# Stacking the query and key operands of an attention stage through scratch memory instead of through on-chip copies

## The chip, the cores and the metric

The kernel runs on one core of one Trainium2 chip. The metric is the device time in microseconds (us). Before the change it is 1969.96 us, the median of three runs (1965.92 to 1970.75). Since there is one core, its span and its clock are the whole picture.

## What is computed

The reference is one gated cross-attention block. Cut to what matters here:

```
x = x + tanh(g_xattn) * attention(layernorm(x), ctx, ctx, heads=16)
x = x + tanh(g_ffn)   * ffn(layernorm(x), w_gate, w_up, w_down)

attention: q, k get rotary position factors;
           scores = q k^T / sqrt(32) + slope[h] * (column - row)
           softmax over columns, times v
ffn:       weights quantized to 4 bits in blocks of 32, activations to 16 bits
```

x and ctx are 4 x 1024 x 512 in float32, with 16 heads of 32 columns each.

## The kernel before

The program is written out engine by engine, with semaphores between them. It has an attention stage (to about 1040 us) and then the feed-forward stages.

Attention works on 16 groups (`p`), each with four heads of one batch element, in the code's words a group's `K` and `Q` parts (`w` = 1 and 0). A group has two halves of 512 query rows, and each half has 8 steps of 128 keys, so a group takes 16 steps (numbered w = 0 to 15 below) and the stage 256. The softmax needs each row's maximum before it starts. So beside the scores of step g (`score`, line 852) TensorE already computes the products for the row maxima of a later half (`row_max`, line 839), 11 steps ahead; VectorE reduces them (line 1205). The maxima of the next group begin at step 5 of this one.

A score is wanted in nearly float32 accuracy, while TensorE gets float16 operands. So q and k are split in a high and a low float16 part (`hi`, `lo`), and the matmul's 101 rows are a stack: rows 0 to 31, 32 to 63 and 64 to 95 hold hi/hi, hi/lo and lo/hi of q and k, rows 96 to 99 the position bias, row 100 the negated maxima. `QA` and `KA` are these stacks.

How a stack comes about: TensorE transposes four heads at once (`turn`, line 826; K of the next group at step 0, Q of the group after the next at step 8). The result has the four heads below each other on 128 partitions. ScalarE writes `hi` (line 1011), VectorE `lo` (line 1220). Then the transfer queue of SyncE moves each head's 32 partitions to the three places in its stack (`stack`, lines 583, 584 and 588): seven transfers a head, at steps 1, 2, 3 and 4 of the group before. `write_rows` (line 595) writes the maxima's row at steps 4 and 12, and they are needed from steps 8 and 0 on. SyncE works strictly in program order, so each of its waits holds back all transfers written behind it.

In `QA` and `KA` there are two sets of buffers, and a set has two tensors with two heads each. A semaphore of a head (`d_st`) tells TensorE that its seven transfers are there.

Of the kernel before, what the change touches and what calls it, by code (L numbers as in the profile page):

```python
# [104 lines left out]
class Step:  # L105


    def __init__(self, g):
        self.g = g
        self.hf, self.s = hf, s = g // 8, g % 8  # L110
        self.p, self.qc = p, qc = hf // 2, hf % 2
        w = 8 * qc + s
        self.inside = 0 <= hf < NHALF
        m = g + 8 + LEAD
        self.hm, self.im = m // 8, m % 8
        self.maxima = 0 <= self.hm < NHALF
# [12 lines left out]
        if 0 <= p and p + 2 < NQ and w in (0, 2, 6, 8, 10, 14):
            k = (0, 2, 6, 8, 10, 14).index(w)  # L130
            self.rope = (p + 2, k // 3, k % 3)
        elif -10 <= g <= -5:
            self.rope = (1, (g + 10) // 3, (g + 10) % 3)
        self.add = hf - 1 if s == 4 and 1 <= hf < NHALF else None
        self.norm = []
        if 2 <= p + 3 < NQ:
            self.norm += [(p + 3, i) for i in NORM_TILES.get(w, ())]
        if g < -7:
            self.norm += [(1, 2 * (g + 11)), (1, 2 * (g + 11) + 1)] if g < -8 else [(1, 6), (1, 7)]
        self.norm.sort()  # L140

        self.load_context = p + 2 if w == 1 and 1 <= p and p + 2 < NQ else None
        self.load_columns = p + 3 if w == 5 and 0 <= p and p + 3 < NQ else None
        self.stack = (p + 1, w - 1) if 0 <= p and 1 <= w <= 4 and p + 1 < NQ else None
        self.rows = self.hm if 0 <= self.hm < NHALF and self.im == 7 else None
        self.store = p - 1 if w == 6 and 1 <= p <= NQ else None

        self.sum = (hf, s // 2) if self.inside and s % 2 == 1 else None
        self.dens = None
        if s % 2 == 1:  # L150
            h, n = (hf, s // 2 - 1) if s > 1 else (hf - 1, 3)
            if 0 <= h < NHALF:
# [120 lines left out]
class Kernel:  # L273


    def __init__(self, nc, ctx, x, ctx_in, gx, gf, wg, wu, wd, cos_d, sin_d, id_d, bias_d, out):
# [48 lines left out]
        self.reach = A("reach", [128, NT, 2], F32)  # L325
        self.xg = [A(f"xg{i}", [128, 8, 128], F32) for i in range(4)]
        self.cg = [A(f"cg{i}", [128, 8, 128], F32) for i in range(3)]
        self.QA = [A(f"QA{i}", [128, 2 * T], F16) for i in range(4)]
        self.KA = [A(f"KA{i}", [128, 2 * T], F16) for i in range(4)]
        self.Pb = [A(f"P{i}", [128, 4, 512], F32) for i in range(NP)]  # L330
        at = A.at - 2 * 8192
        self.bias = nc.alloc_sbuf_tensor_at("bias", [32, T], F32, offset=at)
# [71 lines left out]
        self.d_cg = [sem(f"d_cg{i}") for i in range(3)]  # L404
        self.d_xg = [sem(f"d_xg{i}") for i in range(4)]
        self.d_xl = [sem(f"d_xl{i}") for i in range(NXL)]
        self.d_st = [sem(f"d_st{i}") for i in range(8)]
        self.d_crow = [sem(f"d_crow{i}") for i in range(2)]
        self.d_x2s = sem("d_x2s")
        self.d_wl = [sem(f"d_wl{i}") for i in range(NWL)]  # L410
# [139 lines left out]
def sync_program(e, K):  # L550
# [16 lines left out]
        e.dma_start(K.xl[n % NXL][:, :], K.x_rows[128 * n:128 * n + 128, :]).then_inc(K.d_xl[n % NXL], 16)  # L567


    def stack(p, h):  # L570
        k, a = 2 * (p % 2) + h // 2, h % 2
        r = slice(32 * h, 32 * h + 32)
        c = slice(a * T, a * T + T)
        sem = K.d_st[2 * k + a]
        qd = K.QA[k][:, :].rearrange("p (c a q) -> p a c q", c=2, a=2)[:, a]
        if h == 0:
            e.wait_ge(K.a_hi, turn_no(p, 1 if p else 0, 1))
            e.wait_ge(K.v_lo, turn_no(p, 1 if p else 0, 1))
        if p >= 2 and a == 0:
            e.wait_ge(K.pe_score, score_no(2 * (p - 2) + 1, 7, h + 1))  # L580
        for n, (q, kk) in enumerate(((K.hi, K.hi), (K.hi, K.lo), (K.lo, K.hi))):
            rows = slice(32 * n, 32 * n + 32)
            e.dma_start(qd[rows], q[0][r, :].rearrange("p (c q) -> p c q", c=2)).then_inc(sem, 16)
            e.dma_start(K.KA[k][rows, c], kk[1][r, :]).then_inc(sem, 16)
        if p == 0 and h == 0:
            e.wait_ge(K.d_bias, 48)
            e.wait_ge(K.v_aux, 8)
        e.dma_start(K.KA[k][96:100, c], K.bias_s[4 * (p % 4) + h::NH, :]).then_inc(sem, 16)

    def write_rows(hf):  # L590
        p, qc, k = hf // 2, hf % 2, hf % 2
        e.wait_ge(K.v_row, 4 * hf + 4)
        for j in range(2):
            row = K.QA[2 * (p % 2) + j][100:101, T * qc:T * qc + T].rearrange("o (n q) -> o n q", q=128)
            e.dma_start(row, K.crow[k][8 * j:8 * j + 8, :]).then_inc(K.d_crow[k], 16)

    def load_weight(m, k):
        z, use, old = K.w_buffer(m, k)
# [49 lines left out]
    e.dma_start(K.bias_s[0:32, :], K.biash[0][:, :]).then_inc(K.d_bias, 16)  # L648
    e.wait_ge(K.v_bias, 1)
    e.dma_start(K.bias_s[32:64, :], K.biash[1][:, :]).then_inc(K.d_bias, 16)  # L650
    for h in range(4):
        stack(0, h)
    load_context(2)
    load_x_columns(2)

    for st in STEPS:
        if st.load_context is not None:
            load_context(st.load_context)
        if st.stack is not None:
            stack(*st.stack)  # L660
        if st.load_columns is not None:
            load_x_columns(st.load_columns)
        if st.rows is not None:
# [9 lines left out]
        if st.ffn_loads:  # L673
            for h in range(2):
                for i in range(2):
                    e.wait_ge(K.d_wh[h][i], 16 * 6)
            for k in range(4):
                e.wait_ge(K.d_st[4 + k], 112 * 8)
            for i in range(2):
                e.dma_start(K.Wg[i][:, :, :], K.wt_d[0][i]).then_inc(K.d_Wg, 16)  # L680
            for n in range(NXF):
# [130 lines left out]
def tensor_program(e, K):  # L812
# [15 lines left out]

    def row_max(hm, u, c):
        p, qc, h, qt = hm // 2, hm % 2, u // 4, u % 4  # L830
        j, a = h // 2, h % 2
        k = 2 * (p % 2) + j
        q0 = T * qc + 512 * a + 128 * qt
        use = ("max", hm, u)
        if qc == 0 and u % 4 == 0 and c == 0:
            e.wait_ge(K.d_st[2 * k + a], 112 * (p // 2) + 112)
        if c == 0 or K.bank_release(use, 1) != K.bank_release(use, 0):
            e.wait_ge(*K.bank_release(use, c))
        mm = e.matmul(K.bank(use, c), K.QA[k][0:100, q0:q0 + 128], K.KA[k][0:100, a * T + 512 * c:a * T + 512 * c + 512],  # L839
                      start=True, stop=True)  # L840
        if c == 1:
            mm.then_inc(K.pe_max, 1)

    def score(hf, kt, h):
        p, qc, j, a = hf // 2, hf % 2, h // 2, h % 2
        k = 2 * (p % 2) + j
        n = score_no(hf, kt, h)
        if n > 2:
            e.wait_ge(K.a_exp, n - 2)
        if kt == 0 and h == 0:  # L850
            e.wait_ge(K.d_crow[hf % 2], 32 * (hf // 2) + 32)
        e.matmul(K.score[a], K.KA[k][0:101, a * T + 128 * kt:a * T + 128 * kt + 128],  # L852
                 K.QA[k][0:101, T * qc + 512 * a:T * qc + 512 * a + 512], start=True, stop=True).then_inc(K.pe_score, 1)

    def turn_weight(m, n, ps):
        e.wait_ge(K.g_wq, w_no(m, n))
# [5 lines left out]
    e.wait_ge(K.d_id, 16)  # L862
    for w in (1, 0):
        turn(0, w)
    e.wait_ge(K.v_aux, 8)

    before = None
    for st in STEPS:
# [123 lines left out]
def scalar_program(e, K):  # L992
# [12 lines left out]

    def turned(p, w, half):
        e.wait_ge(K.pe_turn, turn_no(p, w, half))
        if p > 0 and w == 0 and half == 0:
            for h in range(4):
                e.wait_ge(K.d_st[4 * ((p - 1) % 2) + h], 112 * ((p - 1) // 2) + 112)  # L1010
        e.activation(K.hi[w][:, 512 * half:512 * half + 512], K.bank(("turn", p, w), half), ACT.Copy, scale=(QPOW, KPOW)[w]).then_inc(K.a_hi, 1)

    def exponent(hf, kt, h):
# [175 lines left out]
def vector_program(e, K):  # L1189
# [17 lines left out]
    def turn_rows(hm):  # L1207
        e.wait_ge(K.v_max, max_no(hm, 15))
        if hm >= 2:
            e.wait_ge(K.d_crow[hm % 2], 32 * (hm // 2))  # L1210
        for i in range(4):
            e.transpose(K.crow[hm % 2][:, 32 * i:32 * i + 32], K.cm[hm % 2][32 * i:32 * i + 32, :]).then_inc(K.v_row, 1)

    def low_part(p, w, half):
        c = slice(512 * half, 512 * half + 512)
        e.wait_ge(K.a_hi, turn_no(p, w, half))
        if p > 0 and w == 0 and half == 0:
            for h in range(4):
                e.wait_ge(K.d_st[4 * ((p - 1) % 2) + h], 112 * ((p - 1) // 2) + 112)
        e.scalar_tensor_tensor(K.lo[w][:, c], K.bank(("turn", p, w), half), (QPOW, KPOW)[w], K.hi[w][:, c], ALU.mult, ALU.subtract).then_inc(K.v_lo, 1)  # L1220

    def centre_x(n):
# [2 lines left out]
            e.wait_ge(K.g_r2, R2 * (n // 8) + R2)  # L1225
        e.tensor_scalar(K.xf[n % NXF][:, :], K.xf[n % NXF][:, :], K.mv2[:, n, 0:1], K.rs2[:, n:n + 1], ALU.subtract, ALU.mult).then_inc(K.v_xc, 1)

    for i in range(4):
        e.memset(K.KA[i][96:128, :], -1.0).then_inc(K.v_aux, 1)
        e.memset(K.QA[i][96:128, :], QPOW * KPOW).then_inc(K.v_aux, 1)  # L1230
    for i in range(2):
        e.memset(K.cm[i][:, :], 0.0).then_inc(K.v_cm, 1)
    for n in range(8):
# [554 lines left out]
```

## Time and profile before

| | |
|---|---|
| median of three runs | 1969.96 us |
| the profiled execution | 1968.86 us, of which the span is 1967.1 us |
| TensorE busy | 1738.3 us (88%) |
| VectorE busy | 1484.7 us (75%) |
| ScalarE busy | 1187.7 us (60%) |
| GpSimd busy | 898.7 us (46%) |
| transfers of the q and k parts | 384 of 64 KB, and 64 of 8 KB for the bias |

The profile names the engines PE (TensorE, with PEld for its weight loads), DVE (VectorE), ACT (ScalarE), POOL (GpSimd) and SP (SyncE; SPq is its queue, which issues transfers). The time of an SPq row is what the issue takes, not the transfer. What an engine waited for stands in brackets behind its row or in the view of waits. An engine can only be the bound of a stretch in which it is busy nearly throughout, so the stretches have to be looked at one by one.

### The profile page before, as it was taken

To read this page: it belongs to the slowest core of one execution; us is meant where nothing else is said; L and a number is where in the kernel's file an instruction comes from. 1 tells how busy PE (TensorE), PEld (TensorE's weight loads), DVE (VectorE), ACT (ScalarE), POOL (GpSimd) and SP (SyncE) were. 2 spreads that over 40 slices of the span, in tenths; PEclk is the share of its full clock that TensorE was granted. 3 is DMA by queue.
4 is the path that set the end of the run, shared out by engine and by line. 5 is a ranking of instruction groups with operands and counts; after the bars stand their busy time and mean duration, and the time that the engine had idled before them with its cause. 6 is when DMAs were issued, how large, how long until landed. Compare 5 with 4: busy or idle time off the path is not lost. (4 is left out here: it accounts for less than half of the span.)

```text
span 1967.1 us, 26173 instructions
## 1 busy us (share of the span) xinstructions
PE 1738.3 (88%) x9360; PEld 662.5 (34%) x9360; DVE 1484.7 (75%) x2117; ACT 1187.7 (60%) x1911; POOL 898.7 (46%) x411
## 2 busy tenths in 40 slices
PE   1899999999999999999986999999999910299999
PEld 0222333323333323333223554544444400044444
DVE  6899888888787787887845665648999999855442
ACT  2476776777777777666651232228997678854441
POOL 3499999989999999998630010110000000000000
PEclk9999999999999999999997999999999965599999
DMA  4332233112332222221024565547885357755542
GB/s 113 88 115 81 77 87 87 48 49 57 87 88 55 59 61 82 76 56 25 20 97 133 179 204 201 185 153 245 261 269 194 131 178 248 236 186 170 177 161 75
DMA packets 170914, 250.45 MB, mean 127 GB/s; under 512 B 30272, under 2 KB 101312, under 8 KB 170272
## 3 DMA queue, kind: packets, MB, share of 16 engines
q1 hardware_dynamic: 170784, 248.78, 40.2%
q8 instruction: 74, 1.21, 0.3%
q14 instruction: 56, 0.46, 0.1%
HBM read 146.74 MB, written 76.68 MB: 114 GB/s over the span
## 5 line engine op out<-in xcount | busy, mean ns | idle before, releaser
L1024 ACT ACTIVATE P<-quad 128x512 f32<-128x512 f32 x1024 | 557.1, 599 | 243.3 <-PE quad L852 242.9
L1205 DVE TENSOR_REDUCE cm<-quad 128x1 f16<-128x1024 f32 x512 | 601.0, 1216 | 116.5 <-PE quad L839 116.3
L1718 POOL TENSOR_TENSOR Ps<-P,P 128x2048 f32<-128x2048 f32 x124 | 563.0, 4540 | 85.5 <-ACT P L1024 85.3
L852 PE MATMUL quad<-QA,KA 101*128 101x512 f16 x1024 | 352.9, 385 | 6.3 <-ACT P L1024 5.2
L984 PE MATMUL quad<-Wd,oh 128*128 128x512 f16 x768 | 231.6, 382 | 129.5 <-DVE ol L1558 129.5
L839 PE MATMUL quad<-KA,QA 100*128 100x512 f16 x1024 | 323.4, 390 | 24.1 <-issue 7.4
L888 PE MATMUL quad<-P,cg 128*32 128x512 f32 x2048 | 272.7, 604 | 3.6 <-ACT numT L1052 0.6
L1098 ACT ACTIVATE ev<-quad 128x1024 f32<-128x1024 f32 x96 | 97.4, 1015 | 209.6 <-PE quad L945 204.9
L1441 DVE TENSOR_REDUCE mxt<-ev 128x1 f32<-128x1024 f32 x96 | 116.8, 1217 | 113.3 <-ACT ev L1098 113.3
L852 PEld LDWEIGHTS quad<-QA,KA 101*128 101x128 f16 x1024 | 84.2, 97 | 344.8 <-ACT P L1024 233.9
L945 PE MATMUL quad<-x_hi,Wg 128*128 128x512 f16 x768 | 189.2, 381 | 3.6 <-DVE x_lo L1437 3.6
L945 PE MATMUL quad<-x_hi,Wu 128*128 128x512 f16 x768 | 181.9, 379 | 3.3 <-DMA Wu<-wt_scratch 3.3
L984 PEld LDWEIGHTS quad<-Wd,oh 128*128 128x128 f16 x768 | 75.4, 98 | 225.5 <-issue 128.1
L839 PEld LDWEIGHTS quad<-KA,QA 100*128 100x128 f16 x1024 | 98.8, 98 | 153.7 <-DVE lo L1220 25.2
L1693 POOL TENSOR_TENSOR wq<-wl,wsc 128x512 f32<-128x512 f32 x36 | 37.8, 1049 | 243.1 <-DVE wl L1317 243.1
L984 PE MATMUL quad<-Wd,ol 128*128 128x512 f16 x384 | 146.6, 382 | 0.0
L915 PE MATMUL quad<-Ps,ones 128*32 128x512 f32 x1024 | 134.2, 596 | 1.3 <-POOL Ps L1718 0.8
L1126 ACT ACTIVATE sgm<-gq,qs 128x1024 f32<-128x1024 int16 x96 | 109.8, 1146 | 36.7 <-DVE sgq L1486 34.3
L1580 DVE SCALAR_TENSOR_TENSOR xr<-quad,qs,xr 128x512 f32<-128x512 f32 x32 | 24.0, 750 | 122.2 <-PE quad L984 122.2
L945 PEld LDWEIGHTS quad<-x_hi,Wu 128*128 128x128 f16 x768 | 75.0, 98 | 94.4 <-DMA Wu<-wt_scratch 4.3
L945 PEld LDWEIGHTS quad<-x_hi,Wg 128*128 128x128 f16 x768 | 75.2, 98 | 86.8 <-issue 4.2
L945 PE MATMUL quad<-x_lo,Wg 128*128 128x512 f16 x384 | 99.4, 382 | 0.0
(143 smaller groups left out, 2095.7 us busy)
## 6 DMA issues: line engine op xcount, KB each, us to landing
gate_scratch<-ev SPq DMA_DIRECT2D x48, 512.0 KB, 2.9
gt<-gate_scratch SPq DMA_DIRECT2D x48, 512.0 KB, 5.6
up_scratch<-ev SPq DMA_DIRECT2D x48, 512.0 KB, 3.1
uf<-up_scratch SPq DMA_DIRECT2D x48, 512.0 KB, 4.9
uf<-up_scratch SPq DMA_DIRECT2D x96, 256.0 KB, 3.6
wt_scratch<-wh SPq DMA_DIRECT2D x72, 128.0 KB, 2.6
cg<-in_ctx_dram SPq DMA_DIRECT2D x16, 512.0 KB, 3.8
xl<-in_x_dram SPq DMA_DIRECT2D x32, 256.0 KB, 4.4
```

What stands on the lines that cost most here:

```text
L839: mm = e.matmul(K.bank(use, c), K.QA[k][0:100, q0:q0 + 128], K.KA[k][0:100, a * T + 512 * c:a * T + 512 * c + 512], start=True, stop=True)
L852: e.matmul(K.score[a], K.KA[k][0:101, a * T + 128 * kt:a * T + 128 * kt + 128], K.QA[k][0:101, T * qc + 512 * a:T * qc + 512 * a + 512], s ...
L888: mm = e.matmul(K.num[32 * h:32 * h + 32, :], K.cg[p % 3][:, kt, 32 * h:32 * h + 32], K.Pb[before.g % NP][:, h, :], start=kt == 0, stop=kt ...
L915: mm = e.matmul(K.den[32 * h:32 * h + 32, :], K.ones[:, :], K.Ps[n % 2][:, h, :], start=n == 0, stop=n == 3)
L945: mm = e.matmul(K.quad[z][:, 512 * h:512 * h + 512], w_[:, wslot, 128 * c:128 * c + 128], x_[:, c, c0:c0 + 512], start=n == 0, stop=n == 11)
L984: mm = e.matmul(ps, o[k][:, ot, sl], K.Wd[r][:, ot, :], start=m == 0, stop=m == 3 * OT - 1)
L1024: e.activation(K.Pb[pb][:, h, :], K.score[h % 2], ACT.Exp, scale=SCALE / (QPOW * KPOW)).then_inc(K.a_exp, 1)
L1098: e.activation(K.ev[k % NEV][:, :], K.quad[k % nq][:, :], ACT.Copy).then_inc(K.a_ev, 1)
L1126: e.activation(K.sgm[n % NSG][:, :], view(n), ACT.Sigmoid, scale=sg).then_inc(K.a_sig, 1)
L1205: e.tensor_reduce(cm[:, u:u + 1], K.quad[UNIT["max", hm, u] % 2][:, :], AX.X, ALU.max).then_inc(K.v_max, 1)
L1441: e.tensor_reduce(K.mxt[:, col:col + 1], K.ev[k % NEV][:, :], AX.X, ALU.max, apply_absolute_value=True).then_inc(K.v_mx, 1)
L1718: e.tensor_tensor(K.Ps[n % 2][:, :, :], K.Pb[(st.g - 1) % NP][:, :, :], K.Pb[st.g % NP][:, :, :], ALU.add).then_inc(K.g_sum, 1)
```

## The change

The high and low parts are stored to scratch memory as they lie, 256 KB each, by four transfers a group (`store_parts`). From there each of the six blocks of 32 rows is loaded for all four heads at once (`load_stack`, 256 KB each), and the bias in one transfer (32 KB): 11 transfers a group instead of 28. Q is stored at step 9 of the group two before, K at step 1 of the group before; Q and the bias are loaded at step 1 behind K's stores, K at step 2. The maxima's row of a half is one transfer instead of two. A set of `QA` and of `KA` is now one tensor with four heads, one semaphore tells of all seven loads of a group, and TensorE waits for it ahead of a group's first row maxima. VectorE's fills at the start are four of 32x4096 instead of eight of 32x2048. ScalarE and VectorE now wait, before they overwrite a `hi` or `lo`, for the stores (`d_part`), and not for the stack.

```diff
-        self.stack = (p + 1, w - 1) if 0 <= p and 1 <= w <= 4 and p + 1 < NQ else None
+        self.store_parts = None
+        if w == 9 and 0 <= p and p + 2 < NQ:
+            self.store_parts = (p + 2, 0)
+        elif w == 1 and 0 <= p and p + 1 < NQ:
+            self.store_parts = (p + 1, 1)
+        elif g == -2:
+            self.store_parts = (1, 0)
+        self.stack = (p + 1, w - 1) if 0 <= p and 1 <= w <= 2 and p + 1 < NQ else None
...
+        self.part_d = [[nc.dram_tensor(f"part{i}{j}_scratch", shape, F16).ap() for j, shape in enumerate(((2, 2, 128, 512), (2, 1, 128, T)))]
+                       for i in range(2)]
...
-    def stack(p, h):
...
-        for n, (q, kk) in enumerate(((K.hi, K.hi), (K.hi, K.lo), (K.lo, K.hi))):
-            rows = slice(32 * n, 32 * n + 32)
-            e.dma_start(qd[rows], q[0][r, :].rearrange("p (c q) -> p c q", c=2)).then_inc(sem, 16)
-            e.dma_start(K.KA[k][rows, c], kk[1][r, :]).then_inc(sem, 16)
...
+    def store_parts(p, w):
+        e.wait_ge(K.a_hi, turn_no(p, w, 1))
+        if p >= 2:
+            e.wait_ge(K.d_st[p % 2], 112 * (p // 2))
+        dst = [K.part_d[p % 2][w][n].rearrange("c r t -> r c t") for n in range(2)]
+        n = (2, 1)[w]
+        e.dma_start(dst[0], K.hi[w][:, :].rearrange("r (c t) -> r c t", c=n)).then_inc(K.d_part[w], 16)
+        e.wait_ge(K.v_lo, turn_no(p, w, 1))
+        e.dma_start(dst[1], K.lo[w][:, :].rearrange("r (c t) -> r c t", c=n)).then_inc(K.d_part[w], 16)
+
+    def load_stack(p, w):
+        if p >= 2:
+            e.wait_ge(K.pe_score, score_no(2 * (p - 2) + 1, 7, 3))
+        e.wait_ge(K.d_part[w], 32 * p + 32)
+        if p == 0 and w == 0:
+            e.wait_ge(K.v_aux, 4)
+        for n, part in enumerate(((0, 0, 1), (0, 1, 0))[w]):
+            if w == 0:
+                rows = K.QA[p % 2][32 * n:32 * n + 32, :, :, :].rearrange("d c h t -> d (c h) t")
+            else:
+                rows = K.KA[p % 2][32 * n:32 * n + 32, :, :]
+            e.dma_start(rows, K.part_d[p % 2][w][part].rearrange("c (h d) t -> d (c h) t", d=32)).then_inc(K.d_st[p % 2], 16)
+        if w == 0:
...
+            bias = K.bias_s.rearrange("(n h) t -> n h t", h=NH)[:, 4 * (p % 4):4 * (p % 4) + 4, :]
+            e.dma_start(K.KA[p % 2][96:100, :, :], bias).then_inc(K.d_st[p % 2], 16)
...
-        for j in range(2):
-            row = K.QA[2 * (p % 2) + j][100:101, T * qc:T * qc + T].rearrange("o (n q) -> o n q", q=128)
-            e.dma_start(row, K.crow[k][8 * j:8 * j + 8, :]).then_inc(K.d_crow[k], 16)
+        row = K.QA[p % 2][100:101, qc, :, :].rearrange("o h (n q) -> o (h n) q", q=128)
+        e.dma_start(row, K.crow[k][0:16, :]).then_inc(K.d_crow[k], 16)
...
-    for h in range(4):
-        stack(0, h)
+    store_parts(0, 1)
+    store_parts(0, 0)
+    load_stack(0, 1)
+    load_stack(0, 0)
...
-        if qc == 0 and u % 4 == 0 and c == 0:
-            e.wait_ge(K.d_st[2 * k + a], 112 * (p // 2) + 112)
+        if qc == 0 and u == 0 and c == 0:
+            e.wait_ge(K.d_st[p % 2], 112 * (p // 2) + 112)
...
-        if p > 0 and w == 0 and half == 0:
-            for h in range(4):
-                e.wait_ge(K.d_st[4 * ((p - 1) % 2) + h], 112 * ((p - 1) // 2) + 112)
+        if p > 0 and half == 0:
+            e.wait_ge(K.d_part[w], 32 * p)
```

The queue of SyncE at the start of the program, before the change: the first head of the first group (hi0 and lo0 are Q's parts, hi1 and lo1 K's, biash the bias's halves).

```order
L650 DMA bias_scratch<-biash1_103 32x1024 [waits v_bias]
L583 DMA QA0_89<-hi0_145 32x2x512 [waits v_lo,a_hi]
L584 DMA KA0_93<-hi1_146 32x1024
L583 DMA QA0_89<-hi0_145 32x2x512
L584 DMA KA0_93<-lo1_148 32x1024
L583 DMA QA0_89<-lo0_147 32x2x512
L584 DMA KA0_93<-hi1_146 32x1024
L588 DMA KA0_93<-bias_scratch 4x1024 [waits v_aux,d_bias]
```

After these come 21 more for the other three heads. The same place after the change, all four heads:

```order
L669 DMA bias_scratch<-biash1_99 32x1024 [waits v_bias]
L587 DMA part01_scratch<-hi1_142 128x1024 [waits a_hi]
L589 DMA part01_scratch<-lo1_144 128x1024 [waits v_lo]
L587 DMA part00_scratch<-hi0_141 128x2x512 [waits a_hi]
L589 DMA part00_scratch<-lo0_143 128x2x512 [waits v_lo]
L603 DMA KA0_91<-part01_scratch 32x4x1024 [waits d_part1]
L603 DMA KA0_91<-part01_scratch 32x4x1024 x2
L603 DMA QA0_89<-part00_scratch 32x8x512 [waits v_aux,d_part0]
L603 DMA QA0_89<-part00_scratch 32x8x512 x2
L608 DMA KA0_91<-bias_scratch 4x4096 [waits d_bias]
```

What moved: the first head had its stack after seven transfers, now the first and all others have it after eleven, with two waits for stored data between them.

The same queue in the middle of the stage, steps 1 to 4 of a group, after the change (before it, the context load L556 is followed by 28 transfers of the kind above and then by the maxima's rows L595):

```order
L567 DMA cg2_88<-in_ctx_1024_dram 128x8x128 [waits pe_pv]
L587 DMA part01_scratch<-hi1_142 128x1024 [waits d_st0,a_hi]
L589 DMA part01_scratch<-lo1_144 128x1024 [waits v_lo]
L603 DMA QA0_89<-part00_scratch 32x8x512 [waits d_part0,pe_score]
L603 DMA QA0_89<-part00_scratch 32x8x512 x2
L608 DMA KA0_91<-bias_scratch 4x4096
L603 DMA KA0_91<-part01_scratch 32x4x1024 [waits d_part1,pe_score]
L603 DMA KA0_91<-part01_scratch 32x4x1024 x2
L614 DMA QA1_90<-crow1_109 1x16x128 [waits v_row]
```

K's parts of a group are stored and loaded back within these rows, and Q's come from stores made half a group earlier.

## Rows read from the trace of the kernel before

**Rows 1.** The page: busy time of each engine.

```profile
PE 1738.3 (88%) x9360; PEld 662.5 (34%) x9360; DVE 1484.7 (75%) x2117; ACT 1187.7 (60%) x1911; POOL 898.7 (46%) x411
```

**Rows 2.** Windows: stretch, its length, busy PE PEld DVE ACT POOL, clock, DMA, GB/s.

```profile
0.00:74.00 74.00, 26.79 (x68) 8.03 (x69) 53.51 (x62) 15.32 (x33) 28.14 (x32) 1.00 0.38 104
220.00:360.00 140.00, 138.90 (x846) 43.66 (x844) 119.48 (x162) 100.26 (x195) 127.85 (x45) 1.00 0.26 73
```

**Rows 3.** Longest wait of PE, 74 to 1190 us: us, times, longest.

```profile
PE quad L929 <- DVE xf L1431: 13.0, 1, 13.0
```

**Rows 4.** Timeline of the start: start, length, engine, line, operation [idle before <-releaser].

```profile
32.55 1.05 ACT L1011 ACTIVATE hi<-quad 128x512 f16<-128x512 f32 x2
36.35 1.28 DVE L1220 SCALAR_TENSOR_TENSOR lo<-quad,hi 128x512 f16<-128x512 f32 x2
39.12 0.69 DVE L1220 SCALAR_TENSOR_TENSOR lo<-quad,hi 128x512 f16<-128x512 f32 x1 [0.16 <-ACT hi L1011]
44.00 0.47 SPq L588 DMA_DIRECT2D KA<-bias_scratch  x1
45.89 1.86 PE L839 MATMUL quad<-KA,QA 100*128 100x512 f16 x4 [7.44 <-issue]
46.94 19.05 DVE L1205 TENSOR_REDUCE cm<-quad 128x1 f16<-128x1024 f32 x16 [7.13 <-PE quad L839]
```

**Rows 5.** Transfers by kind: count, size of one, us from issue to landing.

```profile
xr<-x_scratch SPq DMA_DIRECT2D x32, 256.0 KB, 2.8
out_dram<-xr SPq DMA_DIRECT2D x32, 256.0 KB, 2.0
```

**Rows 6.** Windows: stack transfers alone; loads into all partitions.

```profile
46.00:57.50 11.50, 9.96 (x20) 1.36 (x18) 10.44 (x9) 0.00 (x0) 10.52 (x6) 1.00 0.38 93
8.50:16.00 7.50, 0.00 (x0) 0.00 (x0) 6.21 (x4) 1.06 (x1) 5.90 (x4) 1.00 1.04 333
```

**Rows 7.** Timeline of VectorE's fills at the start.

```profile
14.07 1.76 DVE L1229 MEMSET KA<- 32x2048 f16 x1 [0.37 <-issue]
16.21 1.76 DVE L1230 MEMSET QA<- 32x2048 f16 x1 [0.38 <-issue]
```

**Rows 8.** Timeline of SyncE's queue, one group and the next's first transfer.

```profile
197.26 0.38 SPq L556 DMA_DIRECT2D cg<-in_ctx_dram  x1
199.80 0.67 SPq L583 DMA_DIRECT2D QA<-hi  x1
203.76 0.48 SPq L588 DMA_DIRECT2D KA<-bias_scratch  x1
217.78 1.39 SPq L595 DMA_DIRECT2D QA<-crow  x2
...
258.13 0.67 SPq L583 DMA_DIRECT2D QA<-hi  x1
```

**Rows 9.** Timeline of PE, same group: steps 4, 5 and then 12, 13.

```profile
210.15 0.60 PE L852 MATMUL quad<-QA,KA 101*128 101x512 f16 x2
213.04 0.60 PE L852 MATMUL quad<-QA,KA 101*128 101x512 f16 x2
213.48 0.81 PE L839 MATMUL quad<-KA,QA 100*128 100x512 f16 x3
...
239.32 0.60 PE L852 MATMUL quad<-QA,KA 101*128 101x512 f16 x2
242.20 0.60 PE L852 MATMUL quad<-QA,KA 101*128 101x512 f16 x2
```

**Rows 10.** Timeline, first group: SyncE's first stack transfer, PE's first row maximum.

```profile
81.01 0.67 SPq L583 DMA_DIRECT2D QA<-hi  x1
93.35 0.81 PE L839 MATMUL quad<-KA,QA 100*128 100x512 f16 x3
```

**Rows 11.** Timeline of DVE: the low part of K at step 0, of Q at step 8.

```profile
198.45 1.29 DVE L1220 SCALAR_TENSOR_TENSOR lo<-quad,hi 128x512 f16<-128x512 f32 x2 [0.77 <-ACT hi L1011]
227.61 1.29 DVE L1220 SCALAR_TENSOR_TENSOR lo<-quad,hi 128x512 f16<-128x512 f32 x2 [0.77 <-ACT hi L1011]
```

More of the change, by code:

```diff
@@ L327, in __init__ @@
         self.cg = [A(f"cg{i}", [128, 8, 128], F32) for i in range(3)]
-        self.QA = [A(f"QA{i}", [128, 2 * T], F16) for i in range(4)]
-        self.KA = [A(f"KA{i}", [128, 2 * T], F16) for i in range(4)]
+        self.QA = [A(f"QA{i}", [128, 2, 4, 512], F16) for i in range(2)]
+        self.KA = [A(f"KA{i}", [128, 4, T], F16) for i in range(2)]
         self.Pb = [A(f"P{i}", [128, 4, 512], F32) for i in range(NP)]
@@ L406, in __init__ @@
         self.d_xl = [sem(f"d_xl{i}") for i in range(NXL)]
-        self.d_st = [sem(f"d_st{i}") for i in range(8)]
+        self.d_part = [sem(f"d_part{i}") for i in range(2)]
+        self.d_st = [sem(f"d_st{i}") for i in range(2)]
         self.d_crow = [sem(f"d_crow{i}") for i in range(2)]
@@ L567, in load_rows @@
         e.dma_start(K.xl[n % NXL][:, :], K.x_rows[128 * n:128 * n + 128, :]).then_inc(K.d_xl[n % NXL], 16)
-    def stack(p, h):
[L571 to L580, printed above, removed]
-        for n, (q, kk) in enumerate(((K.hi, K.hi), (K.hi, K.lo), (K.lo, K.hi))):
-            rows = slice(32 * n, 32 * n + 32)
-            e.dma_start(qd[rows], q[0][r, :].rearrange("p (c q) -> p c q", c=2)).then_inc(sem, 16)
-            e.dma_start(K.KA[k][rows, c], kk[1][r, :]).then_inc(sem, 16)
[L585 to L588, printed above, removed]
+    def store_parts(p, w):
[7 more added lines that the diff above has]
+        e.dma_start(dst[1], K.lo[w][:, :].rearrange("r (c t) -> r c t", c=n)).then_inc(K.d_part[w], 16)
@@ new lines, in load_stack @@
+    def load_stack(p, w):
[11 more added lines that the diff above has]
+        if w == 0:
+            if p == 0:
+                e.wait_ge(K.d_bias, 48)
+            bias = K.bias_s.rearrange("(n h) t -> n h t", h=NH)[:, 4 * (p % 4):4 * (p % 4) + 4, :]
+            e.dma_start(K.KA[p % 2][96:100, :, :], bias).then_inc(K.d_st[p % 2], 16)
@@ L658, in sync_program @@
             load_context(st.load_context)
+        if st.store_parts is not None:
+            store_parts(*st.store_parts)
         if st.stack is not None:
-            stack(*st.stack)
+            load_stack(*st.stack)
         if st.load_columns is not None:
@@ L676, in sync_program @@
                     e.wait_ge(K.d_wh[h][i], 16 * 6)
-            for k in range(4):
-                e.wait_ge(K.d_st[4 + k], 112 * 8)
+            e.wait_ge(K.d_st[1], 112 * 8)
             for i in range(2):
@@ L830, in row_max @@
         p, qc, h, qt = hm // 2, hm % 2, u // 4, u % 4
-        j, a = h // 2, h % 2
-        k = 2 * (p % 2) + j
-        q0 = T * qc + 512 * a + 128 * qt
+        q0 = 128 * qt
         use = ("max", hm, u)
-        if qc == 0 and u % 4 == 0 and c == 0:
-            e.wait_ge(K.d_st[2 * k + a], 112 * (p // 2) + 112)
+        if qc == 0 and u == 0 and c == 0:
+            e.wait_ge(K.d_st[p % 2], 112 * (p // 2) + 112)
         if c == 0 or K.bank_release(use, 1) != K.bank_release(use, 0):
             e.wait_ge(*K.bank_release(use, c))
-        mm = e.matmul(K.bank(use, c), K.QA[k][0:100, q0:q0 + 128], K.KA[k][0:100, a * T + 512 * c:a * T + 512 * c + 512],
+        mm = e.matmul(K.bank(use, c), K.QA[p % 2][0:100, qc, h, q0:q0 + 128], K.KA[p % 2][0:100, h, 512 * c:512 * c + 512],
                       start=True, stop=True)
@@ L844, in score @@
     def score(hf, kt, h):
-        p, qc, j, a = hf // 2, hf % 2, h // 2, h % 2
-        k = 2 * (p % 2) + j
+        p, qc = hf // 2, hf % 2
         n = score_no(hf, kt, h)
@@ L850, in score @@
         if kt == 0 and h == 0:
-            e.wait_ge(K.d_crow[hf % 2], 32 * (hf // 2) + 32)
-        e.matmul(K.score[a], K.KA[k][0:101, a * T + 128 * kt:a * T + 128 * kt + 128],
-                 K.QA[k][0:101, T * qc + 512 * a:T * qc + 512 * a + 512], start=True, stop=True).then_inc(K.pe_score, 1)
+            e.wait_ge(K.d_crow[hf % 2], 16 * (hf // 2) + 16)
+        e.matmul(K.score[h % 2], K.KA[p % 2][0:101, h, 128 * kt:128 * kt + 128],
+                 K.QA[p % 2][0:101, qc, h, :], start=True, stop=True).then_inc(K.pe_score, 1)
     def turn_weight(m, n, ps):
@@ L864, in tensor_program @@
         turn(0, w)
-    e.wait_ge(K.v_aux, 8)
+    e.wait_ge(K.v_aux, 4)
     before = None
@@ L1209, in turn_rows @@
         if hm >= 2:
-            e.wait_ge(K.d_crow[hm % 2], 32 * (hm // 2))
+            e.wait_ge(K.d_crow[hm % 2], 16 * (hm // 2))
         for i in range(4):
@@ L1216, in low_part @@
         e.wait_ge(K.a_hi, turn_no(p, w, half))
-        if p > 0 and w == 0 and half == 0:
-            for h in range(4):
-                e.wait_ge(K.d_st[4 * ((p - 1) % 2) + h], 112 * ((p - 1) // 2) + 112)
+        if p > 0 and half == 0:
+            e.wait_ge(K.d_part[w], 32 * p)
         e.scalar_tensor_tensor(K.lo[w][:, c], K.bank(("turn", p, w), half), (QPOW, KPOW)[w], K.hi[w][:, c], ALU.mult, ALU.subtract).then_inc(K.v_lo, 1)
@@ L1226, in centre_x @@
         e.tensor_scalar(K.xf[n % NXF][:, :], K.xf[n % NXF][:, :], K.mv2[:, n, 0:1], K.rs2[:, n:n + 1], ALU.subtract, ALU.mult).then_inc(K.v_xc, 1)
-    for i in range(4):
-        e.memset(K.KA[i][96:128, :], -1.0).then_inc(K.v_aux, 1)
-        e.memset(K.QA[i][96:128, :], QPOW * KPOW).then_inc(K.v_aux, 1)
+    for i in range(2):
+        e.memset(K.KA[i][96:128, :, :], -1.0).then_inc(K.v_aux, 1)
+        e.memset(K.QA[i][96:128, :, :, :], QPOW * KPOW).then_inc(K.v_aux, 1)
     for i in range(2):
```

## The prediction, made before the changed kernel ran

> **What bounds the kernel now.** I read the page's busy times first. TensorE leads with 1738.3 of 1967.1 us [rows 1], but that is a mean over stages, so I went to the windows. The change touches only the attention stage, up to about 1040 us. There are two kinds of stretch in it [rows 2]. From 220 to 360 us TensorE is busy 138.90 of 140 us, VectorE 119.48 and GpSimd 127.85: TensorE sets the pace. From 0 to 74 us no engine is full (TensorE 26.79 of 74 us, VectorE 53.51): this is a chain that runs once, until the scores start.
>
> Next the waits of TensorE's matmuls in the full part [rows 3]. The longest is one of 13.0 us where the feed-forward stage begins. No row of that view, for 74 to 1190 us, names a stack transfer or a maxima's row as what it waited for. So in the steady part the stack is early, and the question is how early; at the start it may be on the path.
>
> At the start [rows 4]: K's high part is ready at 33.60 us (32.55 + 1.05), K's low part at 37.63 (36.35 + 1.28), Q's low part at 39.81 (39.12 + 0.69). Then the first head is stacked, its last transfer is issued at 44.00, and TensorE's first row maximum starts at 45.89 us after 7.44 us of idle time. From 46.94 us on VectorE makes sixteen row maxima back to back (19.05 us) with 7.13 us of idle time ahead. So what delays 45.89 delays all behind it, one for one.
>
> **The start, with the change.** K's low part is stored at 37.7 us. A 256 KB store lands 2.0 us after its issue and a 256 KB load 2.8 [rows 5]; I take these as the two ends for a store of ours, and 0.38 us for its issue, like the context's [rows 8]. Q's low part is stored at 39.9, and SyncE is free at 40.3. K has landed by then (39.7 to 40.5), so three loads of K are issued from about 40.4 to 42.2 (I take 0.6 us each, near the 0.67 us of a transfer into 32 partitions [rows 8]). Q has landed at 41.9 to 42.7, so three loads of Q go out from about 42.3 to 44.1, and the bias at 44.1.
>
> What bounds the landing? By issue alone, the last load of Q goes out at 43.5 and lands 2.8 us later [rows 5], at 46.3, and the bias, like before, lets TensorE start 45.89 - 44.00 = 1.89 us after its issue, at 46.0. TensorE would start about 46.5: +0.6 us. By data, six loads of 256 KB are 1.57 MB. The stack's own transfers between 46 and 57.5 us moved 93 GB/s at a share of 0.38 of the transfer engines, that is 245 GB/s while they are busy; loads into all 128 partitions reach 333 GB/s [rows 6]. That is 6.4 or 4.7 us, from 40.4, plus 1.9 for the start and the completion: 48.7 or 47.0 us, +2.8 or +1.1. I take 245 GB/s, since these are transfers into 32 partitions as in the row: **+2.8 us**. The worst end is the rate that the stack really had, 93 GB/s, if that was its limit and not the issue of 0.6 us for 64 KB: 16.9 us and a start at 59, +13 us.
>
> The Trainium skill has a rule that speaks against this form (page "SBUF — State Buffer", section "Door 1: The DMA port swizzle"): a transfer into 32 partitions reaches only 8 of 16 ports, with 27.2 GB/s each, about 218 GB/s. The trace agrees in kind, 245 against 333 GB/s, and no run here shows the ports. By that figure the data would take 7.2 us, an estimate, and the start would come 0.8 us later than in my sum.
>
> **The fills.** Eight starts of 32x2048 lie 2.14 us apart, with 1.76 us busy and 0.38 us between [rows 7]. Four of twice the size cost the same if the 2.14 us belong to the columns, and 4 x 0.38 = 1.5 us less if the gap belongs to the instruction. VectorE's statistics start right behind them and lead to Q's parts, so a gain would arrive in full. 2.14 us for 2048 columns is 1.04 ns a column, and the row maxima take 19.05/16 = 1.19 us for 1024, so I hold the rate for the columns' own and take 0. Bounds: -1.5 and 0.
>
> **The steady part, 15 groups.** What was removed was hidden: the first head's last transfer is issued at 203.76 and TensorE wants it at 213.48 [rows 8, 9]. Steps with the stack's transfers beside them are as long as steps without: 213.04 - 210.15 = 2.89 and 242.20 - 239.32 = 2.88 us [rows 9]. So fewer transfers save nothing there. The maxima's rows are written at 217.78, queued behind the stack [rows 8]; they will go some 5 us earlier, but nobody waited for them [rows 3].
>
> What was added has a deadline. K's low part is ready where the stack starts now, 199.80, and TensorE's first row maximum is at 213.48: 13.7 us [rows 8, 9]. In it: the store (0.38 us), Q's three loads and the bias to 202.7 (Q was stored half a group earlier), K's store landing at 201.8 to 202.6, K's three loads issued to 204.6. By data: 1.57 MB of loads and 0.52 MB of stores at 245 GB/s are 8.6 us, plus 1.9: 210.3 us. That leaves **3.2 us**, so no wait. Around the first group the deadline is 93.35 - 81.01 = 12.3 us [rows 10], with one or two row loads of 256 KB in between (1.1 us each), so it is about even there; I put a loss of 0 to 2 us, once, into the range and take 0.
>
> New waits. SyncE now stands at step 9 until Q's low part of step 8 is there. Behind it in its queue are row and weight loads, which are used four and six steps after their place in the order, and the maxima's row of step 12, which waits for VectorE anyway: nothing. ScalarE and VectorE get one wait for stores at step 0, and one instead of four at step 8. VectorE's idle time before the low part is 0.77 us at both today, without such waits and with four [rows 11]: nothing.
>
> **Sum.** 1968.86 (the profiled execution, span 1967.1) + 2.8 + 0 + 0 = 1971.7 us. That execution lies 1.1 us under the median of 1969.96, which gives 1972.8 against the median. I say **1972 us**. A change of 0.3%, 5.9 us, is about what a measurement of this kernel can tell from none, so this is "no change".
>
> **Rivals.**
>
> *K comes late in every group (slower).* If the loads from memory into 32 partitions are slower than the on-chip copies, the 3.2 us run out. It decides at 2.1 MB in 13.7 - 1.9 = 11.8 us, 178 GB/s. For it: K's parts are now stored, waited for and loaded back inside this window, all four heads at once, and TensorE waits for all seven loads before the first head. Against it: 245 GB/s in the row. At 130 GB/s the data take 16.1 us, TensorE waits 4.3 us in each of 15 groups, 65 us, and some 6 us more at the start: about 2040 us. At 165 GB/s, 12.7 us, it is 0.9 x 15 + 3 + 2.8 = 19 us: 1988 us. Chance 0.13.
>
> *The start is bound by issue and the fills get shorter (no change, but a little faster).* +0.6 - 1.5 = -0.9 us: 1968 us. For it: SyncE has 11 issues instead of 28, and the next context and x columns are loaded some 12 us earlier. Against it: 1.57 MB have to arrive before the first matmul, where it was a quarter. Chance 0.17.
>
> *The transfers themselves cost, and fewer of them give time back (faster by more than 0.3%).* The mechanism would be that 28 issues a group hold up something on SyncE's queue: the maxima's row, or the context. If TensorE gained 0.4 us in each of 32 halves (my estimate, the 0.38 us of one issue [rows 8]), it would be 13 us: 1956 us. Against it: no such wait in the rows, and equal steps. The Trainium skill speaks for it (page "DMA: Bandwidth & Descriptors", section "Rules for kernel authors"): coalesce many small transfers, since under 64 KB one pays mostly overhead. By the trace the overhead is real (0.6 us of issue for each 64 KB), but it lies beside TensorE's work. Chance 0.05.
>
> *My forecast*, a start 1 to 6 us later and nothing else: chance 0.65.
>
> **How the numbers follow.** The forecast's cases lie within 5.9 us but for its upper end; with the second they make 0.80 for no change. Slower: the first rival and the forecast's tail, 0.15. Faster: 0.05. The range goes from 1966 (the second rival less the runs' spread) to 1981 (the start at half the way to its worst end, or the first group late as well); it leaves out most of the first rival and the third.
>
> **What would show it.** Right: TensorE's first row maximum at about 48.7 us instead of 45.89, the first score later by as much; groups of 58.3 us in the middle of the stage as before (258.13 - 199.80 [rows 8]); no wait of TensorE for a load of `KA` or `QA` after the first; VectorE's fills 4.2 us apart. Wrong: a wait of TensorE ahead of step 5's row maximum in each group (first rival), the first row maximum before 46 us (second), or a group shorter than 58 us with the step of 2.88 us gone (third).

## The result, and the profile after

The changed kernel takes 1975.01 us (median of 6 runs, 1973.52 to 1977.22), the kernel before 1969.57 us in the same comparison (6 runs). The ratio is 1.003, with a 95% interval of 1.0017 to 1.0042. It is slower by some 5.4 us, 0.3%: just inside the 5.9 us that I had called no change, but clear of noise. I had said 1972 us, range 1966 to 1981. The loss was forecast in sign and place, but it is twice the +2.8 us of the forecast.

The start of the program, from the timeline of the changed kernel (the columns are those of [rows 4]):

```profile
39.82 0.37 SPq L589 DMA_DIRECT2D part_scratch<-lo  x1
40.23 1.47 SPq L603 DMA_DIRECT2D KA<-part_scratch  x3
42.03 1.29 SPq L603 DMA_DIRECT2D QA<-part_scratch  x3
43.37 0.39 SPq L608 DMA_DIRECT2D KA<-bias_scratch  x1
...
51.41 1.87 PE L859 MATMUL quad<-KA,QA 100*128 100x512 f16 x4 [12.97 <-issue]
...
79.87 1.06 PE L871 MATMUL quad<-QA,KA 101*128 101x512 f16 x2
```

SyncE issues all as worked out, the last at 43.37. But the first row maximum starts at 51.41 us instead of 45.89 [rows 4], 5.52 us later, and I had expected 48.7. The first score starts at 79.87 instead of 74.17 (a new row of the kernel before, below), 5.70 later.

Does that difference grow or shrink afterwards? First the kernel before, its first score and its last:

```profile
74.17 0.60 PE L852 MATMUL quad<-QA,KA 101*128 101x512 f16 x2
1023.89 0.88 PE L852 MATMUL quad<-QA,KA 101*128 101x512 f16 x2 [0.47 <-ACT P L1024]
```

Then the changed one: the steps 4 and 5 that answer to [rows 9] (step 5 begins the maxima of group 3, counted from 0), and the last scores.

```profile
215.87 0.60 PE L871 MATMUL quad<-QA,KA 101*128 101x512 f16 x2
218.75 0.60 PE L871 MATMUL quad<-QA,KA 101*128 101x512 f16 x2
219.19 0.81 PE L859 MATMUL quad<-KA,QA 100*128 100x512 f16 x3
...
1029.60 0.88 PE L871 MATMUL quad<-QA,KA 101*128 101x512 f16 x2 [0.47 <-ACT P L1042]
```

219.19 - 213.48 is 5.71 us, and 1029.60 - 1023.89 is 5.71 us. Over 810 us and 13 groups the distance does not change at all. The span grew from 1967.1 to 1973.1 us, so 5.7 of 6.0 us are there before the first score. The other 0.3 us come behind the last score and mean nothing: that unchanged part takes between 941.3 and 945.1 us in the profiles of the nine kernels of this document.

The steady part is not without a trace, though. From the waits of TensorE between 60 and 1190 us, the longest and the one that is new (columns as in [rows 3]):

```profile
PE quad L948 <- DVE xf L1448: 13.0, 1, 13.0
PE quad L859 <- DMA KA<-part_scratch: 1.0, 1, 1.0
```

One wait for a load of K, for the stack whose window I had called about even: group 1's, wanted in step 5 of group 0. Here are the first scores of steps 5 and 6 in the kernel before, and then in the changed kernel with the wait between them:

```profile
92.91 0.60 PE L852 MATMUL quad<-QA,KA 101*128 101x512 f16 x2
96.65 0.61 PE L852 MATMUL quad<-QA,KA 101*128 101x512 f16 x2
```

```profile
97.69 0.60 PE L871 MATMUL quad<-QA,KA 101*128 101x512 f16 x2
99.34 0.82 PE L859 MATMUL quad<-KA,QA 100*128 100x512 f16 x3 [1.05 <-DMA KA<-part_scratch]
102.60 0.61 PE L871 MATMUL quad<-QA,KA 101*128 101x512 f16 x2
```

Step 5 takes 4.91 us instead of 3.74. That the first group is as long as before all the same (59.55 against 59.54 us) is a coincidence: its step 1 is 0.8 us shorter in this profile, for a reason that has nothing to do with the change (last section), and steps 6 and 7 give back 0.2 us.

### The profile page after: what moved, and what is told of

Same layout as the page of the kernel before. It is cut to its first block and busy times, and to the rows that moved or that the text cites. A ratio compares the mean times of both kernels' runs of the same rounds, so it can differ in the third digit from the quotient of the medians.

```text
span 1973.1 us, 25855 instructions
## 1 busy us (share of the span) xinstructions
PE 1740.7 (88%) x9360; PEld 663.0 (34%) x9360; DVE 1485.1 (75%) x2113; ACT 1187.5 (60%) x1911; POOL 898.6 (46%) x411
## 5 line engine op out<-in xcount | busy, mean ns | idle before, releaser
L1188 ACT ACTIVATE uq<-uf,qs 128x512 int16<-128x512 f32 x96 | 68.1, 711 | 52.8 <-DMA uf<-up_scratch 51.4
```

## The experiments

Each was timed beside the kernel before, and the ratios are to that one. The expectations call the kernels by short names; each stands behind its heading. In each, "first row maximum" is the row of TensorE's first product for a row maximum.

### The first group copied on chip (e1)

```diff
-    store_parts(0, 1)
-    store_parts(0, 0)
-    load_stack(0, 1)
-    load_stack(0, 0)
...
+    for h in range(4):
+        copy_head(h, ((0, 0, K.hi), (1, 0, K.hi), (0, 1, K.hi), (1, 1, K.lo), (0, 2, K.lo), (1, 2, K.hi), "bias"))
...
+        if p == 0 and qc == 0 and u % 4 == 0 and c == 0:
+            e.wait_ge(K.d_first[u // 4], 112)
```

> The changed kernel, but the first group's stack is made by the 28 on-chip copies of before, head by head, each head with a semaphore of its own; groups 1 to 15 still go through scratch memory. Theory A (the whole loss is the first group's stack, which the first row maximum waits for): first row maximum back at 45.9 us (51.4 in the changed kernel), every group of 58.3 to 61.9 us as before, total 1969.5, 5.5 us under the changed kernel. Rival B (part of the loss is in the steady part or in the feed-forward stages, through the scratch tensors or the stores): the first row maximum goes back but the total stays at 1972 or more.

```profile
45.80 1.86 PE L873 MATMUL quad<-KA,QA 100*128 100x512 f16 x4 [7.38 <-issue]
```

Measured: 1969.76 us (12 runs) against 1969.88 for the kernel before, ratio 1.0001 (0.9992 to 1.0009, which is 1.7 us either way). With the 28 copies back in one group of 16, the whole loss is gone. The profiles say it more finely: from the first score of group 1 on, every group of this kernel, of the changed one and of the one before has the same length to 0.03 us. So the stores, the 256 KB loads and the new scratch tensors cost nothing there, and nothing that shows in the feed-forward stages. What is left is the wait for group 1's stack, 1.0 us here too. Theory A holds, rival B is out.

### The bias ahead (e2)

```diff
-        if w == 0:
...
+        if w == 0 and p > 0:
...
+    e.wait_ge(K.d_bias, 48)
+    e.wait_ge(K.v_aux, 4)
+    e.dma_start(K.KA[0][96:100, :, :], K.bias_s.rearrange("(n h) t -> n h t", h=NH)[:, 0:4, :]).then_inc(K.d_st[0], 16)
     store_parts(0, 1)
     store_parts(0, 0)
```

> The changed kernel, but the first group's bias (32 KB into four partitions) is loaded ahead of the stores instead of as the last of the eleven transfers. Theory A says that about 1.9 of the 5.5 us are this transfer's tail: the last rows of Q are moved by about 49.1 us, and TensorE starts at 51.4. Then the first row maximum comes at 49.4 to 49.8 us and the total at 1973.2. Rival C (the 2 us are the completion of the last load of Q, or the x and context loads queued behind): 51.4 us as in the changed kernel, total 1975.

```profile
27.23 0.29 SPq L670 DMA_DIRECT2D KA<-bias_scratch  x1
...
49.66 1.86 PE L860 MATMUL quad<-KA,QA 100*128 100x512 f16 x4 [11.24 <-issue]
```

Measured: first row maximum at 49.66, 1.75 us earlier than in the changed kernel; total 1972.42 us (ratio 1.0014, 1.0005 to 1.0022), where I had 1973.2. Rival C is out. So moving the smallest of the seven loads, 32 KB beside six of 256 KB, took back 1.75 of the 5.5 us.

How much of that is the bias's own tail? The semaphore marks in the traces tell when a transfer landed. In the changed kernel the last marks of Q's second load, of Q's third load and of the bias are, by their order, at 48.95, 50.55 and 51.32 us. With the bias ahead, those of Q's two loads are at 48.54 and 49.57. So 0.8 us is the bias landing behind Q's loads, 0.6 us is that Q's third load, its neighbour in the queue, lands later too, and 0.4 us is there before both. The last is a slightly higher rate, here for the changed kernel and then for this one (columns as in [rows 2]):

```profile
42.00:48.00 6.00, 0.00 (x0) 0.00 (x0) 0.00 (x0) 0.14 (x1) 5.71 (x4) 1.00 1.08 222
```

```profile
42.00:48.00 6.00, 0.00 (x0) 0.00 (x0) 0.00 (x0) 0.13 (x1) 5.72 (x4) 1.00 1.08 236
```

The kernels with extra loads below start like the changed one, and their three marks agree with its own to 0.1 us, so the later landing is no accident of one execution of that form. Whether the bias holds up the load in front of it, or the one profile with the bias ahead was quick there, stays open.

### Loaded head by head (e4)

```diff
...
+    for h in range(4):
+        load_head(h, 1)
+        if h == 0:
+            e.wait_ge(K.d_part[0], 32)
+        load_head(h, 0)
```

> The changed kernel, but the first group is loaded from scratch memory head by head (28 loads of 64 KB or less, a semaphore for each head); it is still stored first. This parts the two things that the change did to the start. Theory A (it is that all four heads have to arrive, 1.57 MB at about 205 GB/s): the hop through memory costs next to nothing, because SyncE issues K's loads while Q is stored; first row maximum at 45.5 to 46.5 us, total 1969.5 to 1970. Rival E (storing and loading back is what costs): 49 us or later, total 1973 or more.

```profile
39.81 0.37 SPq L593 DMA_DIRECT2D part_scratch<-lo  x1
40.31 1.36 SPq L614 DMA_DIRECT2D KA<-part_scratch  x3
42.07 1.26 SPq L614 DMA_DIRECT2D QA<-part_scratch  x3
43.37 0.37 SPq L616 DMA_DIRECT2D KA<-bias_scratch  x1
...
45.14 1.86 PE L875 MATMUL quad<-KA,QA 100*128 100x512 f16 x4 [6.71 <-issue]
```

Measured: first row maximum at 45.14, total 1968.07 us (ratio 0.999, 0.9982 to 0.9999). The way through memory is not what costs. Compare the issue times with the changed kernel's above: the same, to 43.37. Only the amount in front of TensorE differs, one head (six loads of 64 KB and the bias) or four. The transfers from memory are even issued faster than the on-chip copies (0.42 us each against 0.6), which makes up for the store: the first head comes 0.75 us earlier than in the kernel before. I had expected 45.5 to 46.5 us and a total of 1969.5 to 1970. Rival E is out.

### K's copies first (e3, and f1 in the kernel before)

This is the version to which the others pointed. K's parts are ready 2 to 6 us before Q's, and all kernels so far let SyncE stand there, or only store.

```diff
...
+    e.wait_ge(K.a_hi, 2)
+    for h in range(2):
+        copy_head(h, ((1, 0, K.hi), (1, 2, K.hi), "bias"))
+    e.wait_ge(K.v_lo, 2)
+    for h in range(2):
+        copy_head(h, ((1, 1, K.lo),))
+    e.wait_ge(K.a_hi, 4)
+    copy_head(0, ((0, 0, K.hi), (0, 1, K.hi)))
+    e.wait_ge(K.v_lo, 4)
+    copy_head(0, ((0, 2, K.lo),))
+    copy_head(1, ((0, 0, K.hi), (0, 1, K.hi), (0, 2, K.lo)))
...
```

> As the kernel whose first group is copied on chip, but in the order in which the parts become ready: K's high rows of two heads and their bias from 33.6 us, K's low rows at 37.7, then Q's three copies of the first head at 39.1 to 41.0. By theory A the time of the first row maximum passes on one for one: its last copy is issued at 40.4, and it starts 1.9 us later at 42.3 instead of 45.9, total 1966.0. Rival D (something behind the first row maximum has slack, like the rotary work of the next group): the first row maximum at 42.3 but the first score less than 3 us earlier than in the kernel before (74.2), total 1968 to 1969.5.

```profile
40.44 0.59 SPq L616 DMA_DIRECT2D QA<-lo  x1
...
42.55 1.86 PE L882 MATMUL quad<-KA,QA 100*128 100x512 f16 x4 [4.13 <-issue]
...
71.21 1.06 PE L894 MATMUL quad<-QA,KA 101*128 101x512 f16 x2
```

Measured: first row maximum at 42.55, first score at 71.21 (2.96 us before that of the kernel before), total 1965.74 us (11 runs; ratio 0.9983, 0.9974 to 0.9991). What is gained before the first row maximum arrives at the end for the most part: 3.34 us there, 2.96 at the first score, 2.56 at the last (below), and 4.1 in the medians. Rival D is out in the total, although the first score stays a hair behind its bound of 3 us.

The same order in the kernel before, with on-chip copies in all groups:

> The kernel before (28 on-chip copies a group throughout), with only the first group's copies put in the order in which the parts become ready, as in e3. Theory A: the steady part does not care how the stacks are made, so this is as fast as e3: first row maximum at 42.5 us, total 1965.5 to 1966.5, with the first group of 59.5 us instead of e3's 60.0, since group 1 gets its first head earlier. A rival (the stack through memory gives something back in the steady part): 1968 or more, two microseconds behind e3.

```profile
42.54 1.86 PE L867 MATMUL quad<-KA,QA 100*128 100x512 f16 x4 [4.09 <-issue]
```

Measured: 1966.09 us (11 runs; ratio 0.9984, 0.9976 to 0.9993). It is as fast as the changed kernel with K's copies first (e3), within the intervals. They beat the kernel before by 4.1 (e3) and 2.7 us (f1), each in its own comparison, and the changed one by some 8 to 9.

The profiles differ more than the medians. The last scores, of e3 and then of f1:

```profile
1021.33 0.88 PE L894 MATMUL quad<-QA,KA 101*128 101x512 f16 x2 [0.47 <-ACT P L1068]
```

```profile
1018.82 0.88 PE L880 MATMUL quad<-QA,KA 101*128 101x512 f16 x2 [0.47 <-ACT P L1052]
```

In f1 they come 2.51 us earlier, and all of it arises up to the end of group 0. From group 1 on, the two have the same lengths to 0.02 us, whether a stack is made by 28 transfers or by 11. In group 0, f1 does not wait for group 1's stack: step 5 takes 3.74 us in it, as in the kernel before, and 4.8 to 5.4 us in the changed kernel and in e1, e2, e3 and e4, which all load that stack from memory. So the merged form has a price of 1.1 to 1.6 us once, at group 1. The rest of the 2.51 us lies before it, mostly in step 0 (3.88 against 5.12 us), where TensorE's matmuls got fast earlier; that can differ without any change (last section). The medians, with intervals of 1.7 us either way, can't confirm the difference.

### How wide the margin of the steady part is (e6, e5)

Ahead of each group's loads of K (from group 1 on) go extra loads of 256 KB into a spare tile: three in one kernel, six in the other (4 runs each). The edit of the kernel with six:

```diff
...
+        if w == 1 and p > 0:
+            if p > 1:
+                e.wait_ge(K.d_spare, 96 * (p - 1))
+            for v in range(2):
+                for n, part in enumerate(((0, 0, 1), (0, 1, 0))[v]):
+                    dst = K.spare[v][32 * n:32 * n + 32, :].rearrange("d (c t) -> d c t", t=(512, T)[v])
+                    e.dma_start(dst, K.part_d[p % 2][v][part].rearrange("c (h d) t -> d (c h) t", d=32)).then_inc(K.d_spare, 16)
```

> The changed kernel, and ahead of each group's three loads of K (from group 1 on) three extra loads of 256 KB into a spare tile that nobody reads. It measures the margin of the steady part. In the changed kernel the last packets of K's loads end at about 215.3 us in group 3, and the row maximum comes at 219.2: 3.8 us. Three loads at 205 GB/s are 3.8 us, so theory A expects the edge: step 5 longer by 0 to 0.5 us in each of 14 groups, by 3.8 in group 1 (which already waits 1 us): total 1979 to 1985. If the margin were much larger than 3.8 us (rival): only group 1 longer, 1979.

> As e6, with six extra loads of 256 KB (7.7 us at 205 GB/s). Theory A: K lands 3.9 us after TensorE wants it, in each of groups 2 to 15, and about 8.5 us in group 1: step 5 of 6.8 us more or less instead of 2.9 + 0.9, groups 3.9 us longer, total 1975 + 14 x 3.9 + 7.7 = 2037 us. The rival of the prediction (K late in every group) is thus made true, and its price can be read: a wait of TensorE for a load into KA, in each group. If other work takes up part of the wait, the total is less than 2037 by that part.

Measured: 1993.55 us with three (ratio 1.0124, 1.011 to 1.0137), 2080.14 us with six (1.0562, 1.0546 to 1.0578). Both are above what I expected (1979 to 1985, and 2037). The waits of TensorE, of the kernel with three and then of the one with six:

```profile
PE quad L871 <- DMA KA<-part_scratch: 17.5, 14, 4.9
```

```profile
PE quad L871 <- DMA KA<-part_scratch: 73.0, 15, 7.0
```

With three, TensorE waits in 14 places, 17.5 us in all: 4.9 us for group 1's stack and about 1.0 us for each of 13 others. So the margin is indeed about as small as the prediction had it: three loads more, some 3.8 us at 205 GB/s, and it is used up in nearly every group. Less the 1.0 us of wait that is left, that makes it about 2.8 us, an estimate, where the prediction had 3.2. With six it waits in all 15, 4.9 us on average, where I had 3.9.

But the waits don't explain the whole loss. Against the changed kernel, the kernel with six has 72 us more of waits (73.0 less 1.0) and loses some 106 us (2080.14 - 1968.75 in its comparison, less the 5.44 of the changed one). The page of each shows where the rest is: TensorE is busy 1775.1 us with six and 1740.7 in the changed kernel, 34.4 us more for the same matmuls, and 72 + 34.4 = 106.4. What that is shows where group 3's maxima begin in the kernel with six:

```profile
234.41 0.60 PE L883 MATMUL quad<-QA,KA 101*128 101x512 f16 x2
239.80 1.46 PE L871 MATMUL quad<-KA,QA 100*128 100x512 f16 x3 [4.79 <-DMA KA<-part_scratch]
241.06 0.63 PE L883 MATMUL quad<-QA,KA 101*128 101x512 f16 x1
...
246.46 0.39 PE L883 MATMUL quad<-QA,KA 101*128 101x512 f16 x1
```

Windows of the same kernel, columns as in [rows 2]:

```profile
236.00:239.80 3.80, 0.00 (x0) 0.00 (x0) 0.00 (x0) 0.00 (x0) 0.39 (x1) 0.61 0.94 207
239.80:243.90 4.10, 4.10 (x14) 1.13 (x18) 2.94 (x5) 1.19 (x2) 0.65 (x1) 0.53 0.89 275
```

After 4.79 us of idle time the granted clock is 0.53 for the next 4.1 us (the lower of the two levels, 1.2 instead of 2.4 GHz), and three row-maximum matmuls take 1.46 us instead of 0.81. A stall of this length is paid twice: by itself, and by the slow matmuls behind it. The kernel with three had 0.38 us of idle time at this place and no slow matmuls behind it. It has one long stall, at group 1's stack, with the same sequel:

```profile
102.98 1.46 PE L871 MATMUL quad<-KA,QA 100*128 100x512 f16 x3 [4.91 <-DMA KA<-part_scratch]
```

Its last score is 19.1 us later than the changed kernel's: 16.5 us of further waits, and most of the other 2.6 us are the slow matmuls behind this one stall.

## Why the prediction was right or wrong

**What bounds.** Right. TensorE sets the pace of the stage, and the groups from 1 on kept their length to a hundredth of a microsecond or two with 17 of 28 transfers gone.

**The start, one for one.** Right in the main. 5.52 us at the first row maximum, 5.70 at the first score, 5.71 at the last. The last agreement is closer than the mechanism: the wait of 1.05 us and the shorter step 1 of group 0 cancel in between. With K's copies first, 3.34 us at the first row maximum came to 2.56 at the last score.

**The size of the start, +2.8 us.** This is the term that was mis-sized; it measured +5.5. Two errors, both in "What bounds the landing?". The first: I took 245 GB/s for the loads, 93 GB/s divided by the share of 0.38 [rows 6]. The changed kernel shows the rate itself, in the first of these windows (the tail of Q's store is in it too):

```profile
41.50:49.00 7.50, 0.00 (x0) 0.00 (x0) 0.00 (x0) 0.64 (x2) 6.71 (x4) 1.00 1.12 217
49.00:51.40 2.40, 0.00 (x0) 0.02 (x1) 0.00 (x0) 0.00 (x0) 2.40 (x2) 1.00 1.18 166
```

217 GB/s, at a share of 1.12. The share can exceed 1 (already in [rows 6], 1.04), so it is no share of the rate, and dividing by it does not give the rate of a full queue. 1.57 MB at 217 are 7.2 us, not 6.4: 0.8 us. The Trainium skill's rule, which I had weighed and set beside the sum (page "SBUF — State Buffer", section "Door 1: The DMA port swizzle"), gives about 218 GB/s for 32 partitions. The 217 lies at it, but with the bias ahead the same loads ran at 236 GB/s from 42 to 48 us, over it. So the trace does not bear the rule out as a bound for several such loads in flight, and what sets the rate was not tried by itself. The second error: I let the bias end with the last load of Q, with 1.9 us for start and completion of the whole as in the kernel before. There it was 8 KB for one head; here it is 32 KB into four partitions, behind 1.57 MB. With it ahead the sum comes out: Q's last load has landed at 49.57 us, and 40.4 + 7.2 + 1.9 is 49.5. With it last, 1.75 us come on top, of which 0.8 us are its own landing. 2.8 + 0.8 + 1.75 = 5.4, and 5.5 were measured. The range held it because its upper end had counted with a rate lower still.

**The fills, 0.** Right. Two starts of the larger fills in the changed kernel:

```profile
5.93 3.47 DVE L1247 MEMSET QA<- 32x4096 f16 x1 [0.80 <-issue]
10.20 3.47 DVE L1246 MEMSET KA<- 32x4096 f16 x1 [0.80 <-issue]
```

4.27 us apart, twice the 2.14 of [rows 7]. The gap grew with the columns as well, from 0.38 to 0.80.

**The steady part, 3.2 us of margin.** Right in the verdict and near in size. The data rates of the changed kernel over group 3's stack:

```profile
210.00:212.00 2.00, 2.00 (x14) 0.59 (x13) 1.51 (x2) 1.67 (x5) 2.00 (x1) 1.00 1.13 216
212.00:214.00 2.00, 2.00 (x14) 0.53 (x13) 1.96 (x2) 1.56 (x3) 2.00 (x3) 1.00 1.08 210
214.00:216.00 2.00, 2.00 (x17) 0.97 (x17) 1.35 (x3) 0.00 (x0) 2.00 (x2) 1.00 0.50 106
216.00:218.00 2.00, 2.00 (x12) 0.66 (x14) 1.06 (x1) 1.71 (x4) 2.00 (x1) 1.00 0.00 0
```

The transfers end in the window from 214 us (a half share), by the packets of the trace at about 215.4, and the row maximum comes at 219.19. The extra loads put the margin at about 2.8 us. Group 1, called about even, waited 1.05 us, and step 5 was 1.2 us longer for it: I had 0 to 2 us in the range and 0 in the sum. In the total it does not show, by luck, as told above.

**New waits, 0.** Right: the kernel with the first group copied (e1) keeps all of them in 14 groups and is as fast as the kernel before.

**Rivals.** "K late in every group" did not come. Its mechanism is real, as the extra loads show, and its prices in the prediction (19 to 65 us) are too low where the waits get long, since they leave out the slow clock behind each: 15 waits of 4.9 us cost some 106 us, where I had 65 for 15 of 4.3. "The start is bound by issue" was wrong: 51.4, not 46.5. "Fewer transfers give time back" was wrong: the kernel with the first group copied and the one before, 1969.76 and 1969.88 us, differ in just that, 11 or 28 transfers in 15 groups, and these groups' lengths agree to 0.03 us.

## What to carry to other kernels

Fewer, larger transfers save nothing where the small ones were issued beside full work, and they cost where the first consumer needed only a part: what TensorE waited for here went from 0.4 to 1.6 MB. In a one-time start, count bytes in front of the first instruction and look at what is last in the queue, however small it is. Then put what is ready early ahead: an order by readiness gained 3 to 4 us where the merge lost 5. And when two profiles agree at the end, look whether they agree on the way: here a wait and a shorter step cancelled.

## What was not expected of the hardware

- A stall of 4.79 us of TensorE is followed by 4.1 us at a granted clock of 0.53, with matmuls at 0.63 us instead of 0.38, and one of 4.91 us likewise; stalls of 0.38, 1.05 and 1.46 us are not.
- Transfers from memory were issued faster than on-chip copies of the same 64 KB: three in 1.24 to 1.37 us, where one copy takes about 0.6.
- When the matmuls get fast at the start differs between profiles of the same work. In the profile of the changed kernel TensorE had left its slow matmuls one step earlier. Its rows at step 1 of group 0, after 0.63 us a matmul in step 0:

```profile
84.99 0.65 PE L871 MATMUL quad<-QA,KA 101*128 101x512 f16 x2
85.48 0.81 PE L859 MATMUL quad<-KA,QA 100*128 100x512 f16 x3
```

In the kernel before, the same pair took 1.06 and 1.49 us there, and so step 1 was 0.8 us longer. That is what paid for most of the longer step 5. It is not the change's doing: the two kernels with extra loads do the same as the changed one up to this point, and their step 1 took 3.15 us (with three) and 3.78 us (with six), against 3.19 in the changed kernel and 4.02 in the kernel before. In the one with six the granted clock fell to 0.50 from 79.9 to 86.6 us. Yet their first row maximum starts at 51.41, 51.39 and 51.43 us. What decides when the matmuls get fast stays open, and there is one profile of each kernel. (The granted clock of a window is printed as 1.00 until the first change that the profile records, also for the stretch from 80 to 85 us of the changed kernel with its matmuls of 0.63 us. At the start, the matmuls' lengths tell the level.)
